# Split q and k parts copied straight from their tile to the stacks, in a ring of three tiles, with an opening in its own order

## The chip, the cores and the metric

The kernel runs on one core of a Trainium2 chip. Times are microseconds (us) of the device. The core has a matrix engine (TensorE, PE in the rows, with its weight loads as PEld), VectorE (DVE), ScalarE (ACT), GpSimd (POOL) and SyncE (SP), which computes nothing and issues transfers. Engines run their own instruction lists in order and wait for each other by semaphores. Transfers (DMA) from SP's queue and from ACT's queue are moved by 16 DMA engines.

## The reference, cut to what matters

Eight sequences of 512 tokens with 256 features. Causal attention with 16 heads of 16 dims, a layer norm, then a routed feed-forward layer (8 experts, each takes 129 tokens of each sequence) and a second layer norm. The change is in how q and k get ready for the scores.

```python
k = proj(W_key)
q = proj(W_query)          # (x @ W.T).reshape(b, t, h, hd).transpose(0, 2, 1, 3) * inv_sqrt_c
v = proj(W_value)
scores = jnp.einsum('bhqd,bhkd->bhqk', q, k) * hd ** (-0.5)
scores = jnp.where(causal, scores, -jnp.inf)
weight = jax.nn.softmax(scores, axis=-1)
out = jnp.einsum('bhqk,bhkd->bhqd', weight, v)
```

## The kernel before, in words

Two programs follow each other: `attention` (up to 491 us) and `experts`. Only `attention` is touched.

For each sequence b, q and k are made in four tiles of 128 rows (dims) by 512 tokens. Tile 4b+n: n % 2 is 0 for q and 1 for k, n // 2 is the half of the heads (8 heads). A `qk` stage is one tile: six passes of 512 columns on PE (L676) into a bank; ACT copies the bank twice, to the first bf16 part (L455) and to fp32, `qk_f` (L456); then POOL (L384 to L386; for sequence 0 DVE, L521 to L523) makes the second and third bf16 parts out of what is left. The three parts are in `parts`, a ring of two tiles that lies in the memory of an expert's second weight matrix (`w_raw` in the rows, as `xt` and `qk_f` do, which lie in that of the first). What is left over after the first part goes through a buffer of its own, `qk_r`.

A score needs for each head its 16 dims times six products of parts as 96 rows: the stacks `qst` and `kst` (`w_parts` in the rows). SP writes the three parts of each tile to DRAM, `part_d` (L316, 3 transfers of 128 KB), and a `stack` stage, which is a half of a sequence, reads them back into the stacks (L327, 12 transfers of 128 KB, each into 16 partitions, in rows of 1 KB). ACT may not write a part before the tile two before has landed in DRAM (`parts_out`, L454).

From the stacks come the `nat` units (L642: scores by query, whose maximum DVE takes in L510; 44 units a sequence, the first 22 need half 0) and the `st` units (L627: scores by key, exponentials by ACT in L430, masked by POOL). `nm` takes the maxima of a half of the heads to three rows of `qst`: DVE cuts them (L540 to L543), PE transposes (L704), ACT copies and issues a transfer of 24 KB from SBUF to SBUF (L470).

The order on all engines is that of `steps()`. An iteration i is 40 slots (g, k), g from 0 to 3, k from 0 to 9: slot (g, k) has an `st` unit of sequence i, one or two `nat` units three quarters of a sequence ahead, and what `STAGES` lists as (g, k, stage, how many sequences ahead, n). The tiles of sequence i+2 stand in slots (0,2), (1,0), (1,7) and (2,2), `stack` for its half 0 in (2,1), for half 1 in (0,1) of the next iteration, and `split`, which cuts the input `xt` of sequence i+3 on ACT (L437) and POOL (L389), in (3,5). SP loads the next `xt` right after `split` (L292). Before a `stack` SP waits until the `st` units of two sequences earlier, in the same half, are done (L323). What comes before iteration 0, the opening, is the same table run with i from -3, where `STARTED` leaves out what has been put in by hand.

PE has two banks each for `st` units and for stages, and three for `nat` units.

## Time and profile before

| | us |
|---|---|
| median of three runs | 966.62 |
| lowest and highest | 963.53, 967.97 |
| the profiled execution | 969.03 |
| its span, first to last instruction | 967.3 |

The span is the one that the rows below show; 1.7 us of the profiled execution lie outside it. In the rows, L12 is line 12 of the kernel before, "x6" a count of instructions, and "[2.58 <-DMA part_d<-w_raw]" says that the engine was idle for 2.58 us ahead of this instruction and what ended it. PEclk is the clock granted to TensorE, 1.00 being 2.4 GHz and 0.50 being 1.2 GHz.

### The profile page before, as it was taken

The page shows a single profiled execution, that of the slowest core. Times are in us where ns is not written, and L with a number is a line of the kernel's source. Part 1 is how long each engine was busy: PE and PEld are TensorE (multiplying, and loading weights), DVE is VectorE, ACT ScalarE, POOL GpSimd, SP SyncE. Part 2 cuts the span into 40 slices and gives each one's busy share as a digit, 9 for nine tenths or more (in the row PEclk, how much of TensorE's full clock was granted, in tenths as well). Part 3 has the DMA queues.
Part 4 walks back from the last instruction along what each step waited for, and adds up shares of the span by engine and source line. Part 5 has one row for each costly group of instructions (what it writes and reads, how often), then busy time and mean ns, then how long its engine had stood idle before and what let it go on. Part 6 is the DMA issues. An engine that isn't in the chain of part 4 may idle for free. (4 is left out here: it accounts for less than half of the span.)

```text
span 967.3 us, 17022 instructions
## 1 busy us (share of the span) xinstructions
PE 836.3 (86%) x5864; PEld 627.4 (65%) x5864; DVE 660.6 (68%) x2017; ACT 520.5 (54%) x1010; POOL 523.2 (54%) x622
## 2 busy tenths in 40 slices
PE   4769999999999999977666999998989899898990
PEld 3444454545455454433365989998989899898990
DVE  4467788787878788999759945555474735546464
ACT  2137666666675757544354445564545556454555
POOL 5347565656565653323655256757375645637344
PEclk9769999999999999988878899999999999998996
DMA  4996767687787778201052224325242332422248
GB/s 140 171 172 122 126 125 149 119 144 140 143 144 144 121 143 177 67 2 45 24 200 81 45 42 89 91 40 131 35 125 45 92 64 51 120 34 33 39 125 257
DMA packets 90102, 100.52 MB, mean 104 GB/s; under 512 B 8736, under 2 KB 83488, under 8 KB 89888
## 3 DMA queue, kind: packets, MB, share of 16 engines
q1 hardware_dynamic: 72560, 77.92, 37.6%
q0 software_dynamic: 12800, 16.92, 10.5%
q10 hardware_dynamic: 4656, 4.59, 1.5%
q8 instruction: 47, 0.77, 0.3%
q14 instruction: 39, 0.32, 0.1%
HBM read 65.38 MB, written 33.62 MB: 102 GB/s over the span
## 5 line engine op out<-in xcount | busy, mean ns | idle before, releaser
L510 DVE CUSTOM_DVE_ANT_0 n_ps<-n_ps,tri 128x512 f32<-128x512 f32 (+3 forms) x512 | 238.5, 517 | 75.3 <-PE n_ps L642 73.8
L1080 DVE TENSOR_TENSOR h_lo<-g,h_hi 128x384 fp32r<-128x384 f32 (+1 forms) x184 | 155.2, 851 | 126.3 <-ACT h_hi L1016 126.0
L430 ACT ACTIVATE pt<-st_ps 128x512 f32<-128x512 f32 x320 | 183.9, 601 | 76.0 <-PE st_ps L627 60.9
L1156 PE MATMUL y_ps<-w_parts,h_hi 128*128 128x256 f32 (+1 forms) x1152 | 213.3, 280 | 0.0
L1011 ACT ACTIVATE g<-h_ps,b 128x384 f32<-128x384 f32 (+1 forms) x192 | 104.2, 543 | 197.8 <-PE h_ps L1142 194.9
L1142 PE MATMUL h_ps<-tt_hi,w_parts 128*128 128x384 f32 (+1 forms) x768 | 179.1, 338 | 32.1 <-issue 21.5
L375 POOL TENSOR_SCALAR_AFFINE_SELECT pt<-pt 128x256 f32<-128x256 f32 (+1 forms) x320 | 111.6, 365 | 130.8 <-ACT pt L430 129.8
L1156 PEld LDWEIGHTS y_ps<-w_parts,h_hi 128*128 128x128 f32 (+1 forms) x1152 | 172.4, 178 | 3.3 <-ACT h_hi L1016 0.2
L983 POOL DMA_INDIRECT acc<-y,tok_no x64 | 102.3, 1599 | 120.6 <-DVE y L1094 112.4
L1156 PE MATMUL y_ps<-w_parts,h_lo 128*128 128x256 f32 (+1 forms) x576 | 161.0, 280 | 0.0
L1142 PEld LDWEIGHTS h_ps<-tt_hi,w_parts 128*128 128x128 f32 x768 | 133.6, 200 | 34.4 <-issue 33.2
L642 PE MATMUL n_ps<-w_parts 96*128 96x512 bf16 (+3 forms) x512 | 127.7, 314 | 15.1 <-DVE nmax L510 12.2
L627 PE MATMUL st_ps<-w_parts 99*128 99x512 bf16 (+3 forms) x512 | 127.0, 310 | 14.2 <-ACT pt L430 12.4
L1156 PEld LDWEIGHTS y_ps<-w_parts,h_lo 128*128 128x128 f32 (+1 forms) x576 | 102.4, 178 | 2.0
L659 PE MATMUL av_ps<-pt,vaug 128*32 128x512 f32 (+3 forms) x1024 | 97.6, 456 | 1.5 <-POOL pt L375 1.5
L1016 ACT ACTIVATE h_hi<-g 128x384 fp32r<-128x384 f32 (+1 forms) x192 | 94.4, 491 | 7.4
L627 PEld LDWEIGHTS st_ps<-w_parts 99*128 99x128 bf16 x512 | 42.6, 99 | 82.8 <-ACT pt L430 49.6
L1142 PE MATMUL h_ps<-tt_lo,w_parts 128*128 128x384 f32 (+1 forms) x384 | 96.1, 333 | 0.0
L642 PEld LDWEIGHTS n_ps<-w_parts 96*128 96x128 bf16 x512 | 44.7, 100 | 49.9 <-DVE nmax L510 34.8
L952 POOL DMA_INDIRECT tok<-x,tok_no x58 | 57.9, 999 | 32.9 <-DVE left_no L1071 16.4
L975 POOL TENSOR_TENSOR w_parts<-w_raw,w_parts 128x2048 fp32r<-128x2048 f32 x14 | 67.6, 4868 | 13.0 <-ACT w_parts L1024 13.0
L510 DVE DVE_READ_ACCUMULATOR2_ANT nmax<- 128x1 f32 x512 | 71.5, 140 | 0.0
(157 smaller groups left out, 1106.1 us busy)
## 6 DMA issues: line engine op xcount, KB each, us to landing
w_parts<-part_d SPq DMA_DIRECT2D x192, 128.0 KB, 6.1
w_raw<-in_w SPq DMA_DIRECT2D x16, 1024.0 KB, 5.6
part_d<-w_raw SPq DMA_DIRECT2D x96, 128.0 KB, 6.1
w_raw<-in_xt SPq DMA_DIRECT2D x8, 512.0 KB, 5.0
res<-in_x SPq DMA_DIRECT2D x8, 512.0 KB, 10.1
x<-res SPq DMA_DIRECT2D x8, 512.0 KB, 7.0
acc<-res SPq DMA_DIRECT2D x8, 512.0 KB, 8.2
fin<-acc SPq DMA_DIRECT2D x4, 512.0 KB, 3.9
```

The costliest lines, as they stand in the source:

```text
L375: nc.gpsimd.affine_select(out=x, in_=x, compare_op=ALU.is_ge, fill=0.0, base=0, pattern=[[0, len(tiles)], [1, P]], channel_multiplier=-1). ...
L430: nc.scalar.activation(pt[:, slot % PT_RING, n % UP, :], st_ps[at % ST_RING][:, :], ACT.Exp, scale=S_SCALE).then_inc(exp_done, 1)
L510: ins = nc.vector.tensor_tensor_reduce(out=src[:, h, :], in0=src[:, h, :], in1=mask, scale=-1.0, scalar=-BIG_NEG, op0=ALU.add, op1=ALU.min ...
L627: ins = nc.tensor.matmul(st_ps[at % ST_RING][:, c:c + T - kb * P], kst[0:KM, b % 2, h, kb * P:(kb + 1) * P], qst[0:KM, b % 2, h, kb * P:T] ...
L642: ins = nc.tensor.matmul(bank[:, j * w:(j + 1) * w], qst[0:KQ, b % 2, h, qb * P:(qb + 1) * P], kst[0:KQ, b % 2, h, 0:w], start=True, stop= ...
L659: ins = nc.tensor.matmul(av_ps[VW * j:VW * (j + 1), n * P:T], vaug[:, seq % 3, n, h, :], pt[:, (seq * PAIRS + h // 2) % PT_RING, u, c:c + ...
L983: nc.gpsimd.indirect_dma_start(acc_d[:, :], bass.IndirectOffsetOnAxis(ap=choice(e, j), axis=0), y[0:rows_of(j), j, :], None, compute_op=AL ...
L1011: nc.scalar.activation(g[:, at % G_RING, 0:cols], h_ps[at % H_RING][:, 0:cols], ACT.Gelu, bias=b1[:, e, n:n + 1]).then_inc(g_done, 1)
L1016: nc.scalar.activation(h_hi[:, q % 2, n, 0:cols], g[:, at % G_RING, 0:cols], ACT.Copy).then_inc(g_hi, 1)
L1080: nc.vector.tensor_tensor(h_lo[:, q % 2, n, 0:cols], g[:, at % G_RING, 0:cols], h_hi[:, q % 2, n, 0:cols].bitcast(F32), ALU.subtract).then ...
L1142: ins = nc.tensor.matmul(h_ps[at % H_RING][:, 0:cols], w[e % 2][:, k, units], x[:, q % TOK_RING, k, 0:cols], start=i == 0, stop=i == len(t ...
L1156: ins = nc.tensor.matmul(y_ps[at % Y_RING][0:rows, 0:C], x[:, q % 2, m, toks], w[e % 2][:, m, :], start=i == 0, stop=i == len(terms) - 1)
```

## The change

1. `part_d`, its 96 writes and the semaphores `parts_out` go. The host sorts the columns of the query and key weights by dim first, then head, inside each half. So the 128 rows of a tile are 16 groups of 8 heads, and a part can go from the tile to 16 partitions of a stack in one transfer. `stack` issues the same 12 transfers of 128 KB, with a tile in SBUF as their source: first the six of part 0 (as soon as ACT has made it), then the other six.
2. `parts` becomes a ring of three tiles (`part_of`; one part of nine has a buffer of its own, `last_part`). ACT may write into it when all 12 transfers of the stack that holds the tile three before have landed.
3. The rest is cut in place: subtract, copy to bf16, subtract (before: subtract, subtract, subtract).
4. In `STAGES` tile 1 moves from (1,0) to (1,2), and tile 3 from (2,2) to (3,1). The load of `xt` is a stage of its own, `xin`, in the place it had.
5. The opening is written out in `opening()` and `OPENING`.

```diff
-ST_RING, N_RING, PT_RING = 2, 3, 4
+ST_RING, N_RING, PT_RING, PART_RING = 2, 3, 4, 3
...
-    (1, 0, 'qk', 2, 1),
     (1, 0, 'onorm', -1, 3),
     (1, 1, 'nmcut', 0, 1),
+    (1, 2, 'qk', 2, 1),
...
-    (2, 2, 'qk', 2, 3),
...
+    (3, 1, 'qk', 2, 3),
...
     (3, 5, 'split', 3, 0),
+    (3, 5, 'xin', 4, 0),
...
+OPENING = {
+    5: (("qk", 1, 0),),
+    2 * N_QUARTER - 1: (("nmcut", 0, 0), ("nm", 0, 0), ("qk", 1, 1), ("stack", 1, 0), ("xin", 2, 0)),
+    2 * N_QUARTER + 3: (("qk", 1, 2),),
+    2 * N_QUARTER + 6: (("v", 1, 0), ("v", 1, 1), ("v", 1, 2), ("v", 1, 3)),
+    3 * N_QUARTER - 1: (("qk", 1, 3),),
+}
...
+    yield "split", 0, 0
+    yield "xin", 1, 0
+    for stage, n in (("qk", 0), ("qk", 1), ("stack", 0), ("centre", 0), ("qk", 2), ("v", 0), ("v", 1), ("v", 2), ("v", 3), ("qk", 3)):
+        yield stage, 0, n
+    yield "split", 1, 0
+    yield "stack", 0, 1
+    yield "fold", 0, 0
+    for n in range(NAT_LEAD * N_QUARTER):
+        yield "nat", 0, n
+        if n in OPENING:
+            yield from OPENING[n]
+    yield "split", 2, 0
+    yield "xin", 3, 0
...
+        j = 3 * (tile % PART_RING) + i
+        return most_parts[:, j, :] if j < 2 * KH * C // T else last_part[:, :]
...
+    def wait_stacked(engine, tile):
+
+        b, half_ = tile // 4, tile % 4 // 2
+        engine.wait_ge(stack_in[half_][b % 2], 16 * BLOCKS * (b // 2 + 1))
...
-                for which, stack, blocks in ((0, qst, Q_PARTS), (1, kst, K_PARTS)):
-                    for at, part in enumerate(blocks):
-                        src = part_d[which, b % 2, part, n, :, :].rearrange("(h d) n -> d h n", d=D)
-                        sp.dma_start(stack[at * D:(at + 1) * D, b % 2, HH * n:HH * (n + 1), :], src).then_inc(stack_in[n][b % 2], 16)
+                for first in (True, False):
+                    for which, stack, blocks in ((0, qst, Q_PARTS), (1, kst, K_PARTS)):
+                        tile = 4 * b + 2 * n + which
+                        if first:
+                            sp.wait_ge(qk_first, tile + 1)
+                        else:
+                            sp.wait_ge(qk_rest, tile + 1)
+                        for at, part in enumerate(blocks):
+                            if (part == 0) == first:
+                                sp.dma_start(stack[at * D:(at + 1) * D, b % 2, HH * n:HH * (n + 1), :],
+                                             part_of(tile, part)).then_inc(stack_in[n][b % 2], 16)
...
-                link(nc.gpsimd.tensor_tensor(qk_r[:, :], qk_f[:, tile % 2, :], parts[:, tile % 2, 0, :], ALU.subtract))
-                link(nc.gpsimd.tensor_tensor(parts[:, tile % 2, 1, :], qk_f[:, tile % 2, :], parts[:, tile % 2, 0, :], ALU.subtract))
-                nc.gpsimd.tensor_tensor(parts[:, tile % 2, 2, :], qk_r[:, :], parts[:, tile % 2, 1, :], ALU.subtract).then_inc(qk_rest, 1)
+                left, mine = qk_f[:, tile % 2, :], [part_of(tile, i) for i in range(3)]
+                link(nc.gpsimd.tensor_tensor(left, left, mine[0], ALU.subtract))
+                link(nc.gpsimd.tensor_copy(mine[1], left))
+                nc.gpsimd.tensor_tensor(mine[2], left, mine[1], ALU.subtract).then_inc(qk_rest, 1)
...
-                    act.wait_ge(parts_out[tile % 2], 48 * (tile // 2))
-                nc.scalar.activation(parts[:, tile % 2, 0, :], ps[:, :], ACT.Copy).then_inc(qk_first, 1)
+                if tile >= PART_RING:
+                    wait_stacked(act, tile - PART_RING)
+                nc.scalar.activation(part_of(tile, 0), ps[:, :], ACT.Copy).then_inc(qk_first, 1)
```

What this does to the order, at the two places that matter. First SP at the start of the opening, tiles 0 to 3 of sequence 0, with the semaphores that each transfer waits for. Before:

```order
7 L316 DMA part_d<-w_raw 128x512 [waits qk_rest,qk_first]
8 L316 DMA part_d<-w_raw 128x512 x2
9 L316 DMA part_d<-w_raw 128x512 [waits qk_rest,qk_first]
10 L316 DMA part_d<-w_raw 128x512 x2
11 L327 DMA w_parts<-part_d 16x8x512 [waits parts_out1,parts_out0]
12 L327 DMA w_parts<-part_d 16x8x512 x11
```

After:

```order
7 L347 DMA w_parts<-w_raw 16x8x512 [waits qk_first]
8 L347 DMA w_parts<-w_raw 16x8x512 x2
9 L347 DMA w_parts<-w_raw 16x8x512 [waits qk_first]
10 L347 DMA w_parts<-w_raw 16x8x512 x2
11 L347 DMA w_parts<-w_raw 16x8x512 [waits qk_rest]
12 L347 DMA w_parts<-w_raw 16x8x512 x2
13 L347 DMA w_parts<-w_raw 16x8x512 [waits qk_rest]
14 L347 DMA w_parts<-w_raw 16x8x512 x2
```

The writes to DRAM and the wait for both tiles are gone; the first three copies wait for ACT's first copy alone.

Second ACT in iteration 1, from slot (1,4) on (`nmt` is the copy of `nm`, `o_t` that of `ot`, `vaug` with `scores` that of a `v`, `pt` an exponential; L455 and L479 are the first copy of a tile). Before:

```order
92 L455 ACTIVATE w_raw<-stage_ps 128x512
93 L456 ACTIVATE w_raw<-stage_ps 128x512
94 L430 ACTIVATE pt<-st_ps 128x512 x5
95 L455 ACTIVATE w_raw<-stage_ps 128x512
96 L456 ACTIVATE w_raw<-stage_ps 128x512
97 L430 ACTIVATE pt<-st_ps 128x512 x3
98 L463 ACTIVATE vaug<-stage_ps 128x16x16
```

After:

```order
92 L479 ACTIVATE w_raw<-stage_ps 128x512
93 L480 ACTIVATE w_raw<-stage_ps 128x512
94 L453 ACTIVATE pt<-st_ps 128x512 x8
95 L487 ACTIVATE vaug<-stage_ps 128x16x16
...
108 L503 ACTIVATE lge<-lg 128x32
109 L453 ACTIVATE pt<-st_ps 128x512 x2
110 L479 ACTIVATE w_raw<-stage_ps 128x512
```

The last tile of a sequence is copied behind the four `v` instead of ahead of them, and the exponentials of the slots after (3,1) stand behind that copy.

## Rows read from the trace of the kernel before

**Rows 1.** The page: the span.

```profile
span 967.3 us, 17022 instructions
```

**Rows 2.** Stages: length, busy us (instructions) of each engine, PEclk, DMA share, GB/s.

```profile
24.00:48.00 24.00, 17.05 (x68) 11.66 (x67) 10.61 (x41) 4.47 (x11) 9.27 (x7) 0.73 1.11 172
48.00:72.00 24.00, 16.52 (x69) 9.59 (x68) 15.74 (x69) 7.42 (x17) 10.01 (x10) 0.63 0.96 171
...
165.30:215.60 50.30, 48.12 (x352) 25.52 (x352) 41.43 (x174) 32.96 (x67) 30.77 (x55) 1.00 0.75 138
...
491.40:967.30 475.90, 419.67 (x3030) 407.57 (x3030) 279.66 (x544) 248.97 (x479) 261.52 (x179) 0.93 0.37 86
```

**Rows 3.** Timeline of the opening: start, us, engine, line, what it writes and reads.

```profile
13.55 0.60 ACT L455 ACTIVATE w_raw<-st_ps 128x512 bf16<-128x512 f32 x1 [5.60 <-PE st_ps L676]
...
20.61 0.17 DVE L529 TENSOR_TENSOR w_lo<-rw,w_hi 128x16 fp32r<-128x16 f32 x1
...
22.23 5.53 SPq L327 DMA_DIRECT2D w_parts<-part_d  x12
...
32.43 1.05 PE L676 MATMUL stage_ps<-xt_lo,w_hi 128*128 128x512 f32 x2
33.28 1.05 PE L676 MATMUL stage_ps<-xt_hi,w_lo 128*128 128x512 f32 x2
...
35.89 0.59 PE L642 MATMUL n_ps<-w_parts 96*128 96x512 bf16 x1 [1.55 <-DMA w_parts<-part_d]
...
36.52 0.70 DVE L510 CUSTOM_DVE_ANT_0 n_ps<-n_ps,tri 128x512 f32<-128x512 f32 x1 [10.93 <-PE n_ps L642]
36.62 0.60 ACT L455 ACTIVATE w_raw<-stage_ps 128x512 bf16<-128x512 f32 x1 [7.81 <-DMA part_d<-w_raw]
...
51.52 0.60 ACT L455 ACTIVATE w_raw<-stage_ps 128x512 bf16<-128x512 f32 x1 [11.36 <-DMA part_d<-w_raw]
...
52.66 0.81 PE L684 MATMUL stage_ps<-w_hi,xt_hi 128*128 128x264 f32 x2 [3.79 <-ACT w_raw L456]
...
70.10 0.14 DVE L510 DVE_READ_ACCUMULATOR2_ANT nmax<- 128x1 f32 x1
...
71.14 1.41 PE L676 MATMUL stage_ps<-xt_hi,w_hi 128*128 128x512 f32 x2
```

**Rows 4.** DMA in five short stretches; columns as in rows 2.

```profile
28.00:34.00 6.00, 2.56 (x6) 1.82 (x6) 0.00 (x0) 0.81 (x1) 2.34 (x1) 0.68 1.15 133
318.00:329.00 11.00, 11.00 (x84) 6.10 (x84) 8.83 (x37) 7.36 (x14) 6.98 (x15) 1.00 1.16 127
169.20:171.80 2.60, 2.60 (x22) 0.54 (x20) 1.98 (x8) 2.11 (x5) 1.86 (x2) 1.00 1.17 152
130.20:131.00 0.80, 0.46 (x6) 0.11 (x3) 0.77 (x3) 0.00 (x0) 0.72 (x2) 1.00 1.09 370
111.90:112.40 0.50, 0.50 (x10) 0.21 (x3) 0.44 (x2) 0.50 (x2) 0.29 (x1) 1.00 0.17 49
```

**Rows 5.** Timeline of iteration 2: SP, PE and ACT around the moved tiles.

```profile
165.69 0.37 SPq L292 DMA_DIRECT2D w_raw<-in_xt  x1
...
166.18 5.61 SPq L327 DMA_DIRECT2D w_parts<-part_d  x12
...
178.01 0.38 PE L642 MATMUL n_ps<-w_parts 96*128 96x512 bf16 x1
...
193.84 5.79 SPq L327 DMA_DIRECT2D w_parts<-part_d  x12
...
205.94 0.34 PE L642 MATMUL n_ps<-w_parts 96*128 96x384 bf16 x1
...
206.93 0.39 PE L642 MATMUL n_ps<-w_parts 96*128 96x512 bf16 x1 [0.39 <-DVE nmax L510]
```

**Rows 6.** Groups, the page's and then 97 to 366 us alone: busy us, mean ns, idle before.

```profile
L510 DVE CUSTOM_DVE_ANT_0 n_ps<-n_ps,tri 128x512 f32<-128x512 f32 (+3 forms) x512 | 238.5, 517 | 75.3 <-PE n_ps L642 73.8
...
L384 POOL TENSOR_TENSOR w_raw<-w_raw 128x512 f32<-128x512 f32 x21 | 24.3, 1158 | 38.9 <-ACT w_raw L456 29.4 <-ACT w_raw L455 9.6
```

More of the change, by code:

```diff
@@ L93 @@
 ROUND_AT += [(B, place) for place in (1, 5, 12, 16)]
-STARTED = [(-2, stage, n) for stage in ("qk", "v", "stack") for n in range(4)]
-STARTED += [(-1, "stack", 0), (-1, "nmcut", 0), (-1, "nm", 0)]
 AV_PLACES = (4, 5, 6, 7)
@@ L99, with opening @@
 BY_DVE = ("onorm", "proj", "pick", "picked")
+OPENING = {
[5 more added lines that the diff above has]
+}
+def opening():
+    yield "split", 0, 0
[11 more added lines that the diff above has]
+    yield "xin", 3, 0
 def steps():
-    for i in range(-3, B + 1):
+    yield from opening()
+    for i in range(B + 1):
         for g in range(4):
@@ L118, in steps @@
                     yield "av", group, AV_PLACES.index(k)
-                if (i, g, k) == (-2, 0, 0):
-                    for stage, n in (("qk", 0), ("qk", 1), ("stack", 0), ("centre", 0), ("qk", 2), ("qk", 3), ("v", 0), ("v", 1), ("v", 2), ("v", 3)):
-                        yield stage, 0, n
-                if (i, g, k) == (-1, 2, 0):
-                    yield "fold", 0, 0
                 for gg, kk, stage, ahead, n in STAGES:
-                    if (gg, kk) == (g, k) and 0 <= i + ahead < B and (i, stage, n) not in STARTED:
+                    if (gg, kk) == (g, k) and 0 <= i + ahead < B:
                         yield stage, i + ahead, n
-                        if (i, stage, n) == (-1, "qk", 1):
-                            yield "stack", 1, 0
                 place = 10 * g + k
@@ L269, in attention @@
     bases = sem("bases")
-    part_d = nc.dram_tensor("part_d", [2, 2, 3, 2, P, T], BF16).ap()
     act_no, dve_no = numbers(BY_ACT), numbers(BY_DVE)
@@ L298, in _ @@
         for stage, b, n in steps():
-            if stage == "split" and b + 1 < B:
-                sp.wait_ge(x_split, b + 1)
-                load_xt(b + 1)
-                if b == 0:
+            if stage == "xin":
+                sp.wait_ge(x_split, b)
+                load_xt(b)
+                if b == 1:
                     sp.dma_start(wpn[:, :, :], wpn_d.rearrange("(k p) n -> p k n", p=P)).then_inc(wpn_in, 16)
@@ L331, in _ @@
                     sp.wait_ge(qk_rest, 4 * B)
+                    for half_ in range(2):
+                        wait_stacked(sp, 4 * (B - 1) + 2 * half_)
                     sp.dma_start(ahead["w1_raw"][:, :, :], w1_d[0].rearrange("(k p) n -> p k n", p=P)).then_inc(ahead["w1_in"], 16)
@@ L518, in _ @@
                     dve.wait_ge(qk_rest, n)
[L519 to L523 removed]
+                left, mine = qk_f[:, n % 2, :], [part_of(n, i) for i in range(3)]
+                link(nc.vector.tensor_tensor(left, left, mine[0], ALU.subtract))
+                link(nc.vector.tensor_copy(mine[1], left))
+                nc.vector.tensor_tensor(mine[2], left, mine[1], ALU.subtract).then_inc(qk_rest, 1)
             elif stage == "centre":
```

29 lines of the change are left out of this document (6 added, 23 removed).

## The prediction

> **What bounds the kernel now.** First the page's head and a table of stages [rows 1, 2]: of a span of 967.3 us, the experts take 475.9 from 491.4 on, and nothing in them is touched. In an iteration in the middle of the attention (165.3 to 215.6 us) PE is busy for 48.1 of 50.3 us at full clock: PE is the bound, with about 2 us of idle time an iteration. DVE has 41.4, ACT 33.0, POOL 30.8. The 16 DMA engines are used at 0.75, and no engine waits for a transfer there. In the opening it is otherwise: from 24 to 72 us PE is busy for 33.6 of 48 us, at a clock of 0.73 and 0.63, and the DMA share is 1.11 and 0.96.
>
> Then the timeline of the opening [rows 3]. The reader is to see three waits. The first stack is read from 22.23 us on, and PE's first `nat` unit gets it at 35.89, so DVE makes its first maximum only at 36.52. ACT waits 7.81 and 11.36 us for parts to land in DRAM, behind stack transfers in the same queue. While it does, PE waits 3.79 us for a stage bank. DVE ends the 33 units of the opening at 70.24, and PE begins the first tile of sequence 2, the first work that needs the next input, at 71.14.
>
> Last the transfers [rows 4, 5]: they decide what the new wait of ACT costs.
>
> **The change, part by part.**
>
> *Less traffic.* 96 writes of 128 KB go, 12.6 MB. In the middle nobody waits for them, so they are worth nothing there beyond what they take from the queue ahead of stacks. In the opening they are the waits of 7.81 and 11.36 us.
>
> *The stack transfers themselves.* Twelve are left, with another source. In stretches in which the queue holds stack reads, the engines move 133, 127 and 152 GB/s with all 16 busy; rows of the same 1 KB size for `res`, which go to 128 partitions, run at 370 GB/s [rows 4]. So it is neither the size of the rows nor DRAM as a source that makes them slow, and what is left that sets them apart is that 16 partitions take them. That speaks for the same rate when the source is SBUF. At 128 KB each: 0.86 us at 152 GB/s, 0.99 at 133, 1.03 at 127. The one copy from SBUF to SBUF, that of `nm`, speaks for more: 24 KB on 3 of 16 engines (share 0.17) at 49 GB/s [rows 4], which is 16 GB/s an engine where a stack read gives 8 to 9.5. It is short, though, and may end before whatever slows the others fills up. From first issue to release the first stack took 35.89 - 22.23 = 13.7 us, of which 12 x 0.99 = 11.9 are transfers and 1.8 start and completion [rows 3, 4]. I take release = first issue + 1.8 + 12 d, with d = 0.86 us: with the part writes gone the queue holds less beside the stacks, as in the stretch with 152 GB/s. The ends of d are SP's issue at 5.6 / 12 = 0.47 [rows 5] and 1.03.
>
> The Trainium skill bears on this twice. "SBUF — State Buffer", section "Door 1: The DMA port swizzle", says that a transfer's bandwidth goes by how many of 16 ports its partitions reach; 16 partitions in a row reach four of them, a quarter of 436 GB/s, an estimate of 109 GB/s and 1.2 us for each transfer. By that rule every wait below would be 2 to 4 us longer. "DMA: Bandwidth & Descriptors", section "Where 436 GB/s comes from", says that copies inside SBUF are held by the fabric at 435 GB/s and not by memory; by that the transfers would keep up with SP. The rows at 127 to 152 GB/s stand near the first, the `nm` copy nearer to the second.
>
> *The new wait of ACT, tile 1 in slot (1,2).* It needs the stack of half 1 of the sequence before. Iteration 2 [rows 5]: SP issues `xt` at 165.69, the stack from 166.18. `xt` goes first in the queue, 512 KB at 370 GB/s, 1.4 us, of which 0.5 is SP's own distance: 0.9. Release: 166.18 + 0.9 + 1.8 + 12 x 0.86 = 179.2. ACT wants the tile when PE has done it: the unit of slot (1,2) ends at 178.2, 1.6 us of that was the tile which now stands behind it, so PE again ends at 178.2, and ACT comes at 178.3. Wait 0.9 us. Behind it on ACT are the exponentials of slot (1,3) and on; PE has two banks and some 0.4 us of other work ahead. Cost 0.5 us. At d = 0.99 it is 2.0, at 1.03 2.5, under 0.78 nothing. It comes in iterations 1 to 4; in iteration 5 no `xt` goes ahead and there is hardly a wait. In iteration 0 the stack is issued only after `split` of sequence 2, later against the slots: 2 us (0 to 4).
>
> *Tile 3 in slot (3,1)* needs half 0 of its own sequence, issued at 193.84: release 193.84 + 1.8 + 10.3 = 205.9. PE ends the unit of (3,1) at 206.1, ACT comes at 206.2: no wait. At d = 0.99 it is 1.3 us, at 1.03 1.8, in each of 6 iterations. Tiles 0 and 2 need stacks that have landed by then (tile 2: five slots behind tile 1).
>
> Sum of the waits at 0.86: 4 x 0.5 + 2 = 4 us.
>
> *The moved tiles.* PE's work is the same. At (3,1) PE now waits for DVE twice, 0.39 us (at 206.93) and about as much two units later; a tile of 1.4 us there fills these, and POOL, without a tile at (2,2), gives DVE its `rstd` sooner. Against that DVE, busy for 41 of 50 us, has less time at (2,2). Where ACT's wait stops PE, DVE catches up too. I take -0.5 us for each of 6 iterations, -3 (0 to -6).
>
> *Cutting in place.* One POOL subtraction of 1.16 us [rows 6] becomes a cast. Bound: 0 to -1.1 us for each tile on POOL, which is not the bound. It is counted only in the opening's DVE chain, at nothing.
>
> *The opening.* The first stack copies go out when ACT has made tile 0's first part, at 13.55 + 0.60 = 14.15 instead of 22.23; the last three need DVE's cut of tile 1, which stands ahead of L529 (20.61) in DVE's order, so all twelve are out by about 21 [rows 3]. From 15 on (the first input and weight loads are ahead of them; I take 1 us for that) the stack needs 10.3 us and 1.1 to complete: 26.5, or 28 at d = 0.99. That isn't what comes last now. The four `v` stand ahead of tile 3 and wait for L529, which ends at 20.78. A pair of passes of 512 columns at half clock starts 0.85 us after the one before (32.43, 33.28), so a tile is 2.9 us with its end, a `v` with 264 columns 1.3; at full clock half of that, 1.45 and 0.7. PE is through tile 3 at 25.5 to 29. ACT's three copies, 2.2 us, and POOL's part of `split`, 2.35 as for twice the columns of [rows 6], line two, give the next input at 30 to 33.6; before, PE had it at 31.4: no gain. DVE cuts tile 3 and begins its maxima at about 31.5, 5 us sooner than at 36.52. The 33 units are 12 heads; 128 heads took 238.5 us [rows 6], 1.86 each, 22.3. DVE is stopped three times by PE's new order: by tile 0 of sequence 1, by the transpose of the maxima with tile 1 in a row, and by four `v` in a row: at full clock some 1.6 + 2.6 + 1.8 us, at half clock 1.6 + 4.1 + 4.1, with 1.2 for cutting the maxima. It ends at 31.5 + 22.3 + 1.2 + 6.0 = 61.0, or 64.8, against 70.24. But the last tile now stands at the very end: PE 1.4, ACT 1.1, POOL three steps of 1.16, less for the cast, 3.1, then POOL's 2.35. So the first tile of sequence 2 can start at 61.0 + 8.0 = 69.0, against 71.14. Gain 2 us; at half clock it is a loss of 2, and with fewer stops a gain of 5. What is late next is POOL with tile 3 and `split`.
>
> **Sum.** -2 (opening) - 3 (moved tiles) + 4 (ACT's waits) = -1: 969.03 - 1 = 968.0 in an execution like the profiled one, whose span and 1.7 us around it move together. That execution is 2.4 us above the median; in terms of the median 965.6, and I say 965.5. Its own range is 960 to 971.
>
> **The rivals.**
>
> *A, the copies inside SBUF keep up with SP.* d is under 0.75, ACT never waits for a stack. For it: the `nm` copy at twice the rate an engine, and `res` at 370 GB/s. Against it: 16 receiving partitions as before. The opening is then worth 3 and the moved tiles 3.5. Time: -6.5, so 962.5 and 960.1 by the median; range 956 to 963.
>
> *B, slower: ACT's wait for the stack becomes the bound.* d is 0.99 to 1.03, as most of the stack reads show. The wait at (1,2) costs 2.0 to 2.5 in four iterations and 3.5 in iteration 0, 12.5 in all; that at (3,1) 1.3 to 1.8 in six, 9; sum 21.5. Less 5 for idle time of PE and DVE that these stops swallow and 2 for the opening: +14.5, so 983.5 and 981 by the median; range 971 to 990. It decides from about d = 0.88 us, where the waits are worth more than the gains. For it: [rows 4], lines one and two. Against it: the line with 152 GB/s.
>
> *C, the opening gains nothing.* PE's gaps keep the clock at 0.5 as in [rows 2], and POOL's chain at the end eats the rest: 3 to 4 us more than forecast, 969 by the median; range 965 to 973.
>
> **How the numbers follow.** Chances: forecast 0.36, A 0.27, B 0.28, C 0.09. A measurement of this kernel can tell about 0.5% from no change, 4.8 us: faster is below 961.8, slower above 971.5. Faster: A 0.24, forecast 0.09: 0.33. Slower: B 0.28, C 0.02, forecast 0.03: 0.33. The same: 0.34. The likeliest is the forecast's 965.5. Range 956 to 984: it holds all but the far end of B and some of A.
>
> **What would show it.** In the trace of the changed kernel: DVE's first maximum at 31 to 32 us; no wait of ACT for a stack in the opening beyond 1 us; the first tile of sequence 2 on PE at 69. In iterations 1 to 4 ACT's first copy of tile 1 "<-DMA w_parts" with about 1 us, tile 3 with none; 2.4 and 1.3 us or more mean B, none at all means A. An iteration, 50.3 us before [rows 2], should be 50.3 again, 50 for A and 53 for B. The GB/s while stack copies alone are in the queue give d directly. The experts should take 475.9 us again; if they don't, the forecast is wrong in a place that it doesn't look at.

## The result, and the profile after

| | us |
|---|---|
| changed kernel, median of four runs | 996.79 (995.29 to 1003.04) |
| kernel before, beside it | 966.19 |
| ratio | 1.0331, 95% interval 1.0281 to 1.0381 |
| span of the profiled execution, before and after | 967.3, 995.0 |

The change makes the kernel slower by 3.3%, and the time is outside the range of 956 to 984. The page of the changed kernel, its span and two of the groups of [rows 6]:

```profile
span 995.0 us, 16861 instructions
...
L534 DVE CUSTOM_DVE_ANT_0 n_ps<-n_ps,tri 128x512 f32<-128x512 f32 (+3 forms) x512 | 239.0, 519 | 102.9 <-PE n_ps L665 100.8
...
L407 POOL TENSOR_TENSOR w_raw<-w_raw 128x512 f32<-128x512 f32 x28 | 32.4, 1157 | 98.5 <-ACT w_raw L479 72.6
```

The work costs what it did (maxima 519 ns for 517, the subtraction 1157 ns for 1158), but DVE now waits 100.8 us for PE's `nat` units, where it waited 73.8. The stages, to be held against [rows 2] (length, busy us and count of PE, PEld, DVE, ACT, POOL, then PEclk, DMA share, GB/s); the third is an iteration, 50.30 us long before, and the last ends the experts:

```profile
24.00:48.00 24.00, 17.11 (x69) 10.51 (x69) 16.36 (x53) 4.92 (x13) 5.26 (x4) 0.71 0.95 107
48.00:72.00 24.00, 16.12 (x77) 10.04 (x78) 13.47 (x60) 7.38 (x18) 7.54 (x8) 0.78 0.51 72
...
179.36:235.78 56.42, 50.50 (x356) 26.57 (x352) 40.32 (x172) 32.83 (x67) 28.63 (x54) 0.94 0.63 95
...
520.00:995.00 475.00, 418.89 (x3030) 406.83 (x3030) 277.81 (x544) 249.43 (x479) 262.54 (x179) 0.93 0.36 86
```

Two marks in both traces place the loss: ACT's first copy of the first tile of sequence 2, and its `nmt` copy in slot (3,4) of iteration 5, called the mark from here on (the expectations below speak of the last maxima). Behind the mark lie what is left of the attention and the experts.

| | before | after | difference |
|---|---|---|---|
| start to first tile of sequence 2 | 74.30 | 78.71 | +4.4 |
| from there to the mark | 287.30 | 311.33 | +24.0 |
| from the mark to the end | 605.70 | 604.96 | -0.7 |

The iterations lose most. ACT's waits between 72 and 395 us (engine, line, waited for: us, times, longest):

```profile
ACT w_raw L479 <- DMA w_parts<-w_raw: 21.1, 4, 7.9
...
ACT w_raw L479 <- DMA w_parts<-last_part: 10.2, 2, 6.2
```

These are the six first copies of tile 1 in slot (1,2), 31.4 us together, one in each of the iterations 0 to 5. One of them, with SP, ACT and PE in order of time (against [rows 5]), and then the stretches around it:

```profile
182.86 0.37 SPq L316 DMA_DIRECT2D w_raw<-in_xt  x1
183.34 5.10 SPq L347 DMA_DIRECT2D w_parts<-w_raw  x8
...
191.76 0.60 SPq L332 DMA_DIRECT2D res<-in_x  x1
...
200.83 0.60 ACT L479 ACTIVATE w_raw<-stage_ps 128x512 bf16<-128x512 f32 x1 [6.12 <-DMA w_parts<-w_raw]
...
202.46 0.61 PE L650 MATMUL st_ps<-w_parts 99*128 99x512 bf16 x1 [4.19 <-ACT pt L453]
```

```profile
195.00:200.00 5.00, 3.27 (x24) 1.58 (x22) 3.66 (x17) 0.00 (x0) 0.19 (x1) 1.00 1.14 132
200.00:203.00 3.00, 0.54 (x2) 0.13 (x2) 0.00 (x0) 2.17 (x5) 0.95 (x1) 0.82 0.30 82
203.00:206.00 3.00, 3.00 (x15) 1.21 (x14) 0.76 (x2) 0.93 (x2) 2.83 (x6) 0.50 0.03 8
206.00:209.00 3.00, 3.00 (x18) 1.46 (x16) 0.62 (x2) 1.26 (x3) 0.41 (x1) 0.55 0.00 0
```

The reader is to see a chain of four. The stack lands 17.5 us after its first issue; ACT, which came at 194.7, does nothing until then; PE stands still for 4.19 us behind ACT's exponentials; and when it starts again, the granted clock is at 0.50, 1.2 GHz, for some 6 us. So the stop is paid for again: PE is busy for 50.50 us in this iteration, where the same work takes 47.60 in the run with a ring of four below. Not all of ACT's 6.12 us is the stack's. PE finishes the tile only at 196.2, and in the ring of four ACT waits at the same copy, for PE alone:

```profile
181.74 0.60 ACT L481 ACTIVATE w_raw<-stage_ps 128x512 bf16<-128x512 f32 x1 [1.56 <-PE stage_ps L701]
```

The opening, against [rows 3]:

```profile
13.73 6.92 POOL L420 MEMSET w_parts<- 3x8192 f32 x1
...
14.29 20.12 SPq L347 DMA_DIRECT2D w_parts<-w_raw  x20
...
15.59 5.35 DVE L545 CAST w_raw<-w_raw 128x512 bf16<-128x512 f32 x1
...
21.76 0.60 ACT L479 ACTIVATE w_raw<-st_ps 128x512 bf16<-128x512 f32 x1 [5.33 <-DVE w_raw L546]
...
30.64 0.60 ACT L479 ACTIVATE w_raw<-st_ps 128x512 bf16<-128x512 f32 x1 [1.10 <-DMA w_parts<-w_raw]
...
32.81 2.34 POOL L412 TENSOR_TENSOR xt_lo<-w_raw,xt_hi 128x1024 fp32r<-128x1024 f32 x1 [12.16 <-ACT xt_hi L460]
32.99 2.71 DVE L546 TENSOR_TENSOR w_raw<-w_raw 128x512 bf16<-128x512 f32 x1
...
35.71 0.68 DVE L534 CUSTOM_DVE_ANT_0 n_ps<-n_ps,tri 128x512 f32<-128x512 f32 x1
...
69.06 0.60 ACT L479 ACTIVATE w_raw<-stage_ps 128x512 bf16<-128x512 f32 x1 [5.03 <-DMA w_parts<-last_part]
...
75.78 1.19 PE L699 MATMUL stage_ps<-xt_hi,w_hi 128*128 128x512 f32 x2 [3.14 <-POOL xt_lo L412]
```

The first copies do go out at 14.29, as predicted. But DVE's cast of 512 columns takes 5.35 us (0.43 us for the next one), so tile 2 is copied at 21.76 (at 17.57 in the run without casts below); a subtraction takes 2.71 instead of 0.69; and at the end ACT waits 5.03 us for stack (1,0) before it may write the last tile. The first maximum is at 35.71, not 31.5, and the first tile of sequence 2 on PE at 75.78, not 69. That GpSimd's memset holds a cast on DVE could have been read from the kernel before. There the cast of 128x16 ended at 20.57 and the memset at 20.54; in the changed kernel the same cast, behind the memset, takes 0.17 us.

```profile
13.61 6.93 POOL L397 MEMSET w_parts<- 3x8192 f32 x1
...
19.54 1.03 DVE L528 CAST w_hi<-rw 128x16 fp32r<-128x16 f32 x1
```

### The profile page after: what moved, and what is told of

Same layout as the page of the kernel before. It is cut to its first block and busy times, and to the rows that moved or that the text cites. A ratio compares the mean times of both kernels' runs of the same rounds, so it can differ in the third digit from the quotient of the medians.

```text
span 995.0 us, 16861 instructions
## 1 busy us (share of the span) xinstructions
PE 839.2 (84%) x5864; PEld 626.2 (63%) x5864; DVE 657.0 (66%) x2017; ACT 519.9 (52%) x1010; POOL 508.5 (51%) x622
## 3 DMA queue, kind: packets, MB, share of 16 engines
q10 hardware_dynamic: 4656, 4.59, 1.4%
## 5 line engine op out<-in xcount | busy, mean ns | idle before, releaser
L534 DVE CUSTOM_DVE_ANT_0 n_ps<-n_ps,tri 128x512 f32<-128x512 f32 (+3 forms) x512 | 239.0, 519 | 102.9 <-PE n_ps L665 100.8
L1103 DVE TENSOR_TENSOR h_lo<-g,h_hi 128x384 fp32r<-128x384 f32 (+1 forms) x184 | 132.4, 728 | 126.8 <-ACT h_hi L1039 126.6
L665 PE MATMUL n_ps<-w_parts 96*128 96x512 bf16 (+3 forms) x512 | 128.6, 316 | 17.5 <-DVE nmax L534 15.6
L682 PE MATMUL av_ps<-pt,vaug 128*32 128x512 f32 (+3 forms) x1024 | 101.5, 472 | 2.0 <-POOL pt L398 2.0
L407 POOL TENSOR_TENSOR w_raw<-w_raw 128x512 f32<-128x512 f32 x28 | 32.4, 1157 | 98.5 <-ACT w_raw L479 72.6
L665 PEld LDWEIGHTS n_ps<-w_parts 96*128 96x128 bf16 x512 | 44.7, 100 | 52.2 <-DVE nmax L534 37.9
```

Of the source, the lines that this page charges most:

```text
L534: ins = nc.vector.tensor_tensor_reduce(out=src[:, h, :], in0=src[:, h, :], in1=mask, scale=-1.0, scalar=-BIG_NEG, op0=ALU.add, op1=ALU.min ...
L665: ins = nc.tensor.matmul(bank[:, j * w:(j + 1) * w], qst[0:KQ, b % 2, h, qb * P:(qb + 1) * P], kst[0:KQ, b % 2, h, 0:w], start=True, stop= ...
L682: ins = nc.tensor.matmul(av_ps[VW * j:VW * (j + 1), n * P:T], vaug[:, seq % 3, n, h, :], pt[:, (seq * PAIRS + h // 2) % PT_RING, u, c:c + ...
L1103: nc.vector.tensor_tensor(h_lo[:, q % 2, n, 0:cols], g[:, at % G_RING, 0:cols], h_hi[:, q % 2, n, 0:cols].bitcast(F32), ALU.subtract).then ...
```

## The experiments

The theory after the traces, **W**: the loss is ACT's wait for a stack, in slot (1,2) above all. Rivals: **T**, the copies inside SBUF slow the engines or each other; **M** or its opposite, that the moved tiles cost or bring something; and for the size of the wait, whether source, order, receiving partitions or rows set the rate of a copy.

**A ring of four tiles.** The fourth lies in a buffer that `attention` doesn't use until its end.

```diff
-ST_RING, N_RING, PT_RING, PART_RING = 2, 3, 4, 3
+ST_RING, N_RING, PT_RING, PART_RING = 2, 3, 4, 4
...
+        if j >= 9:
+            return ahead["tok0"][:, :, :].rearrange("p a c -> p (a c)").bitcast(BF16).rearrange("p (j n) -> p j n", n=T)[:, j - 9, :]
```

> The changed kernel with a ring of four tiles of parts instead of three, so that a tile waits for the stack that holds the same tile of the sequence before, which has landed long ago. Theory W (the loss is ACT's wait for a stack): in the changed kernel these waits are 7.93, 6.23, 6.12, 4.59, 4.01 and 2.48 us at tile 1 and 5.03 us at the last tile of the opening, and 23.8 us were lost between the start of iteration 0 and the last maxima. Without the waits an iteration is back at 50 to 50.5 us (53.8, 55.3, 56.4, 54.7 with them) and the time is about 970, or 967 if the opening gets back its 4 to 5 us too. Rival T (the traffic itself: copies inside SBUF slow PE, DVE or ACT): the waits go but an iteration stays at 53 or more, time 985 to 995. The rate of the copies should not change under either.

Measured: 965.89, ratio 0.9993 (0.9978 to 1.0008). No wait of ACT for a stack is left, and an iteration (columns as above) is

```profile
214.16:263.46 49.30, 47.60 (x356) 25.58 (x352) 40.32 (x172) 32.85 (x68) 28.64 (x54) 1.00 0.73 109
```

W holds, T falls. Since both kernels begin the iterations at the same time (`split` of sequence 2 at 70.28), the price of each wait can be read by itself. The length goes from one `split` to the next, the last one to the mark:

| iteration | 0 | 1 | 2 | 3 | 4 | 5 |
|---|---|---|---|---|---|---|
| ACT's wait in the changed kernel | 7.93 | 6.23 | 6.12 | 4.59 | 4.01 | 2.48 |
| at the same copy in the ring of four, for PE's tile | 1.34 | 1.55 | 1.56 | 1.55 | 1.55 | 1.55 |
| length, changed kernel | 53.79 | 55.29 | 56.42 | 54.73 | 51.50 | 48.03 |
| length, ring of four | 45.22 | 49.33 | 49.33 | 49.30 | 49.32 | 47.40 |
| price of the wait | 8.6 | 6.0 | 7.1 | 5.4 | 2.2 | 0.6 |
| of which PE is busy for longer | -0.4 | 1.6 | 2.9 | 2.8 | 0.1 | 0.1 |
| PEclk, changed kernel | 0.87 | 0.97 | 0.94 | 0.94 | 1.00 | 1.00 |
| PEclk, ring of four | 0.86 | 1.00 | 1.00 | 1.00 | 1.00 | 1.00 |

31.4 us of waits cost 29.9, of which 1.9 in iteration 0 come before its wait (the first tile of sequence 2 is at 78.71 instead of 76.84, late from the opening). The stack's own share of a wait is row one less row two. In iterations 1 to 5 the price is that share, less 0.37 us that PE has in hand, plus what PE's work takes longer at the lower clock. So a share of 2.46 us costs 2.2 in iteration 4, at full clock, and one of 3.04 costs 5.4 in iteration 3, of which 2.8 is clock.

**Another order of the copies.** From sequence 1 on, neighbours go to different blocks of 16 partitions.

```diff
+                if b:
+                    sp.wait_ge(qk_rest, 4 * b + 2 * n + 2)
+                    for which, at in ((0, 0), (0, 1), (0, 4), (0, 5), (1, 0), (1, 1), (1, 4), (1, 5), (0, 2), (0, 3), (1, 2), (1, 3)):
...
```

 Theory O (each copy is held by the ports of its 16 partitions, and neighbours overlap only where these differ): the first issue of a stack to ACT's release falls from 15.3 to 17.6 us to 12 or less, the waits at tile 1 from 4 to 8 us to 0 to 3, and the time from 996.8 to 972 to 985. Rival F (a copy is slow by itself, by the source or by the size of its rows, and they go one after another): 15 to 17.6 us again and a time within 3 us of 996.8.

Measured: 996.92, 1.0320 (1.0297 to 1.0344). The time is rival F's, and a miss for theory O; but two things hide in it. In the opening stack (1,0) now waited for the cut of both its tiles, and ACT for it 11.53 us instead of 5.03. Behind that the iterations were 5.5 us shorter. The run was repeated without that part, the spread order only from stack (1,1) on:

> The changed kernel with the copies of a stack in the spread order, for stack (1,1) and all later ones; the first three stacks as in the changed kernel. In the first run of that order the opening lost 7 us, because stack (1,0) then waited for the cut of tile 1, and the iterations gained 5.5 (319.8 to 314.2 us from the last `split` of the opening to the last maxima). Theory: the gain alone, 5 to 6 us, time 990 to 993. Rival: no gain, 996 to 998.

Measured: 989.99, 1.0223 (1.0163 to 1.0283), at the edge of the theory's 990 to 993. The waits at (1,2) sum to 28.8 instead of 31.4. One iteration, with a wait of 4.79 us, keeps its clock:

```profile
176.92:229.16 52.24, 47.65 (x356) 25.60 (x352) 40.31 (x172) 32.70 (x67) 28.58 (x54) 1.00 0.65 103
```

The next, with 5.86 us, takes 54.81 at 0.97. From the last `split` of the opening to the mark this kernel is 5.6 us shorter than the changed one; 2.6 of it is waiting, and in iterations 1 to 4 PE is busy for 2.6 us less, which is clock. The order itself is worth about half a microsecond a stack.

**The copies by themselves.** Twelve copies of 128 KB behind the kernel's last instruction, one series after the other:

> The kernel before, and behind its last instruction eight series of twelve transfers of 128 KB with nothing else running, each series waited for before the next: from SBUF in the changed kernel's order of blocks; from SBUF in the order of the kernel before (0, 16, 32, 48, 64, 80, twice); from DRAM in that order; from DRAM in the changed kernel's order; from SBUF in the order 0, 16, 64, 80, 0, 16, 64, 80, 32, 48, 32, 48; from SBUF with all twelve into the same 16 partitions; from DRAM likewise; from SBUF into 128 partitions. Theory O (ports of the receiving partitions, overlap only between neighbours that differ): about 14 to 15 us for all twelve into the same partitions whatever the source, 10 to 12 in the order of the kernel before, less in the spread order, 13 to 15 in the changed kernel's order, 4 to 8 into 128 partitions. Theory S (the source makes the difference): 14 to 15 for every series from SBUF and 10 to 11 for every one from DRAM. Rival R (a rate of 0.86 us a copy as I predicted, slower in the changed kernel only because other traffic shares the queue): 10 to 11 us for all the series into 16 partitions.

The time from the first issue of a series to that of the next, which waits for all twelve, and the rate in its middle:

| into | from | order of blocks | us | GB/s |
|---|---|---|---|---|
| 16 partitions | SBUF | changed kernel's | 15.3 | 118 |
| 16 | SBUF | kernel before's | 14.8 | 121 |
| 16 | DRAM | kernel before's | 13.8 | 130 |
| 16 | DRAM | changed kernel's | 13.7 | 133 |
| 16 | SBUF | spread | 14.9 | 123 |
| 16 | SBUF | all the same | 16.7 | 105 |
| 16 | DRAM | all the same | 16.5 | 105 |

Two of these series in the trace (columns as in [rows 4]), in turn and all into the same 16 partitions:

```profile
976.00:982.00 6.00, 0.00 (x0) 0.00 (x0) 0.00 (x0) 0.00 (x0) 0.00 (x0) 0.50 1.16 118
...
1045.00:1055.00 10.00, 0.00 (x0) 0.00 (x0) 0.00 (x0) 0.00 (x0) 0.00 (x0) 0.50 1.17 105
```

No theory is right as a whole. The source makes 1.0 or 1.6 us of 15 and, where all copies go to the same partitions, 0.2; the order makes half a microsecond, and the same partitions every time make 2. In the first 1.5 us in which a series moves data, stretches of half a microsecond reach 190 to 242 GB/s, and the rest runs at 105 to 133, so a rate from the first microseconds of a stack is too high. Two queues at once:

> The kernel before, and behind its last instruction six series of twelve copies of 128 KB from SBUF into 16 partitions, issued half by SyncE's queue and half by ACT's: one block of partitions each (0 and 16; then 0 and 80; then 0 and 0), the six blocks in turn on both, and blocks 0, 64, 32 against 16, 80, 48; at the end all twelve on SyncE's queue, in turn. On one queue twelve copies took 14.8 us in turn and 16.7 into the same partitions. Theory K (the receiving ports bound it): two blocks of different ports at once take 8 to 10 us, the same block twice 16 to 17. Rival J (the 16 DMA engines bound it, each row costs its time whatever its partition): 14 to 17 us for all.

```profile
970.00:980.00 10.00, 0.00 (x0) 0.00 (x0) 0.00 (x0) 0.00 (x0) 0.00 (x0) 0.50 1.15 121
...
999.00:1011.00 12.00, 0.00 (x0) 0.00 (x0) 0.00 (x0) 0.00 (x0) 0.00 (x0) 0.50 1.16 105
```

The first row is partitions 0 to 15 from one queue and 16 to 31 from the other, 15.0 us; the second is 0 to 15 from both, 16.7 us. With the six blocks in turn on both queues it was 115 GB/s. K's 8 to 10 us didn't come. The number of receiving partitions and the length of the rows:

> The kernel before, and behind its last instruction five series of twelve copies of 128 KB from SBUF on SyncE's queue: into 16 partitions (128 rows of 1 KB, six blocks in turn, as before: 14.8 us); into 32 partitions, then 64, then 128, the same rows of 1 KB; last into 16 partitions again in rows of 4 KB, read from 32 partitions. Theory K (ports of the receiving partitions): 32 partitions take 8 to 9 us, 64 no less, 128 9 as measured (there SyncE issues no faster), rows of 4 KB 14 to 16. Rival R (each row of 1 KB costs an engine its time): 32 and 64 partitions 14 us as well, rows of 4 KB 8 to 10.

```profile
972.00:981.00 9.00, 0.00 (x0) 0.00 (x0) 0.00 (x0) 0.00 (x0) 0.00 (x0) 0.50 1.15 121
986.00:994.00 8.00, 0.00 (x0) 0.00 (x0) 0.00 (x0) 0.00 (x0) 0.00 (x0) 0.50 1.14 143
999.00:1006.00 7.00, 0.00 (x0) 0.00 (x0) 0.00 (x0) 0.00 (x0) 0.00 (x0) 0.50 1.16 154
1010.00:1016.00 6.00, 0.00 (x0) 0.00 (x0) 0.00 (x0) 0.00 (x0) 0.00 (x0) 0.50 0.59 198
1021.00:1029.00 8.00, 0.00 (x0) 0.00 (x0) 0.00 (x0) 0.00 (x0) 0.00 (x0) 0.50 1.05 130
```

16, 32, 64 and 128 partitions in rows of 1 KB, then 16 in rows of 4 KB: 14.9, 12.9, 12.2 and 9.3 us for the first four. Up to 64 partitions all engines are busy; at 128 they are busy for 0.59 only, and SP, at 0.64 us a copy, is the bound. Long rows bring little. So what holds a copy goes with how many partitions receive it, but not in proportion, and what it is stays open.

**Cutting without a cast**, on DVE (shown) and likewise on GpSimd:

```diff
-                link(nc.vector.tensor_tensor(left, left, mine[0], ALU.subtract))
-                link(nc.vector.tensor_copy(mine[1], left))
+                link(nc.vector.tensor_tensor(mine[1], left, mine[0], ALU.subtract))
+                link(nc.vector.tensor_tensor(left, left, mine[0], ALU.subtract))
```

> The changed kernel with the rest cut by three subtractions again, in place (second part = left - first, then left = left - first, then the third), so that no engine casts. Theory L (DVE's cast of 5.35 us at 15.59 in the changed kernel waits for GpSimd's memset, which ends at 20.65; a subtraction there took 0.69 us in the kernel before): the cast's place takes 0.7 us, the first copy of tile 2 on ACT comes at 17 to 18 instead of 21.76, the first maximum at 31 to 32 instead of 35.71. The time falls by 0 to 4 us, less if the opening is then held by ACT's wait for stack (1,0). Rival (the cast waits for something else, a semaphore or a late input): the same 5 us stand at the first subtraction.

Measured: 1000.62, 1.0366 (1.0337 to 1.0395).

```profile
15.72 0.69 DVE L545 TENSOR_TENSOR w_raw<-w_raw 128x512 f32<-128x512 f32 x1
...
17.57 0.60 ACT L479 ACTIVATE w_raw<-st_ps 128x512 bf16<-128x512 f32 x1 [0.76 <-PE st_ps L699]
...
30.14 0.60 ACT L479 ACTIVATE w_raw<-st_ps 128x512 bf16<-128x512 f32 x1 [3.79 <-DMA w_parts<-w_raw]
...
32.76 2.71 DVE L546 TENSOR_TENSOR w_raw<-w_raw 128x512 bf16<-128x512 f32 x1
...
35.48 0.68 DVE L534 CUSTOM_DVE_ANT_0 n_ps<-n_ps,tri 128x512 f32<-128x512 f32 x1
```

Theory L is right on the cast: in its place stands 0.69 us, and tile 2 comes at 17.57. It is wrong on the maximum, 35.48. The 4 us are waited away at tile 3, which needs the first stack, landed 15.7 us after its first issue. The time, forecast to fall by up to 4 us, didn't: the median is 3.8 us above the changed kernel's, and the two intervals overlap. The waits at (1,2) were 33.4 us instead of 31.4; why they are longer is open.

**Tile 1 later, in the ring of three.**

```diff
-    (1, 2, 'qk', 2, 1),
...
-    (1, 7, 'qk', 2, 2),
+    (1, 6, 'qk', 2, 1),
...
+    (2, 2, 'qk', 2, 2),
```

> The changed kernel, its ring of three and its opening, with tile 1 in slot (1,6) instead of (1,2) and tile 2 in (2,2) instead of (1,7). A stack is landed some 15.5 to 18 us after its `xt` is issued, ACT comes to slot (1,2) at 11.9 us, and a slot is 1.23 us. Theory W (only the wait in the wrong place costs): at (1,6) the wait is 0 to 1.5 us, an iteration 49.3 to 50.5, time 966 to 972, with the opening's loss still in it. Rival (what stands behind the tiles is then late: the third stage bank's turn, `stack` in (2,1), GpSimd): an iteration is 51 or more, time 976 or more.

Measured: 971.20, 1.0023 (0.9999 to 1.0047). A wait of 3.14 us is left in iteration 0 and none later, and an iteration takes 49.80 us. From the last `split` of the opening to the mark it is 295.5 us, against 319.8 in the changed kernel and 289.9 with the ring of four: four slots give back 24 of the 30 us, without any memory. With the opening's two small mends beside it:

> As the last, with DVE's three subtractions and with the input of sequence 2 loaded behind stack (0,1). Both mend something in the opening that ACT's waits for stacks cover in a ring of three (3.79 us at tile 3 of sequence 0 and 5.55 at the last tile, in the run without casts). Theory C (covered): within 2 us of the run before it. Rival: the opening gains 3 to 6 us as with the ring of four.

Measured: 969.21, 1.0020 (0.9996 to 1.0043): covered, as expected. The first tile of sequence 2 is copied at 78.09 instead of 78.56.

**One part alone on the kernel before.** The moved tiles:

```diff
+        table = STAGES if i < 0 else MOVED
```

> The kernel before, parts through DRAM, with tile 1 in slot (1,2) and tile 3 in slot (3,1) from iteration 0 on, nothing else. With the ring of four an iteration takes 49.33 us against 50.35 in the kernel before. Theory M (the moved tiles are the cause): 49.3 to 49.5 here too, time 960 to 963. Rival N (it is the cast on GpSimd, 0.61 for 1.16 us, or the 96 writes that are gone): 50.3 us, time 965 to 968.

Measured: 963.37, 0.9944 (0.9918 to 0.9970).

```profile
211.84:261.17 49.33, 47.63 (x356) 25.59 (x352) 40.36 (x172) 32.84 (x67) 30.67 (x55) 1.00 0.76 141
```

The moved tiles alone take 1.0 us off an iteration, with all the traffic through DRAM still there (141 GB/s against 109 above). Theory M; the 12.6 MB and the cast are worth nothing there. What the moved tiles give can be read from DVE, which is busy for 40.36 us instead of 41.46. Before, GpSimd cut tile 1 (from 178.39 to 182.11 in iteration 2) while DVE cut the maxima for `nm`, and two small casts waited; with tile 1 in (1,2) GpSimd comes to it later. Before, then here:

```profile
178.81 0.77 DVE L540 CAST nm<-nmax 128x32 bf16<-128x32 f32 x1
...
179.84 1.02 DVE L542 CAST nm<-nmax_r 128x32 bf16<-128x32 f32 x1
```

```profile
228.49 0.18 DVE L575 CAST nm<-nmax 128x32 bf16<-128x32 f32 x1
...
228.93 0.18 DVE L577 CAST nm<-nmax_r 128x32 bf16<-128x32 f32 x1
```

PE's waits for maxima, the gain that the prediction named, fall from 0.8 to 0.4 us an iteration. How much of the 1.0 us is one and how much the other no run tells, since both tiles were moved together. Then the order of the opening:

> The kernel before, parts through DRAM and a ring of two, with the changed kernel's order of the opening, nothing else. Theory G (the order itself holds the opening: one tile at the very end and the input of sequence 2 loaded behind stack (1,0)): the first tile of sequence 2 is copied 2 to 5 us later than in the kernel before (74.30), time 968 to 972. Rival H (the order is sound, and what the changed kernel lost there is its cast and its ring of three): 74 or earlier, time 961 to 967.

Measured: 981.46, 1.0116 (1.0069 to 1.0164), worse than expected.

```profile
70.24 0.43 SPq L308 DMA_DIRECT2D w_raw<-in_xt  x1
...
79.66 1.06 ACT L453 ACTIVATE xt_hi<-w_raw 128x1024 fp32r<-128x1024 f32 x1 [11.86 <-DMA w_raw<-in_xt]
```

The new order puts the load of sequence 2's input behind stack (1,0) in SP's list, and SP waits there for that stack's tiles. In the changed kernel ACT's wait for the stack covers it; with the ring of four it shows as 2.36 us.

**A mended opening, with the ring of four.** DVE cuts without the cast, tile 3 stands ahead of the four `v`, and the load of the input behind stack (0,1).

```diff
-    for stage, n in (("qk", 0), ("qk", 1), ("stack", 0), ("centre", 0), ("qk", 2), ("v", 0), ("v", 1), ("v", 2), ("v", 3), ("qk", 3)):
+    for stage, n in (("qk", 0), ("qk", 1), ("stack", 0), ("centre", 0), ("qk", 2), ("qk", 3), ("v", 0), ("v", 1), ("v", 2), ("v", 3)):
...
     yield "stack", 0, 1
+    yield "xin", 2, 0
```

> The ring of four tiles, and the opening mended where its traces show waits: DVE cuts by three subtractions (no cast behind the memset), tile 3 of sequence 0 is made ahead of the four v (in the ring of four it needs no stack), and the input of sequence 2 is loaded behind stack (0,1) instead of behind stack (1,0). With the ring of four alone DVE's first maximum was at 35.75 us and ACT's copy of the first tile of sequence 2 at 76.84, against 36.52 and 74.30 in the kernel before. Theory P (the opening is a chain through DVE, begun by the first stack, which lands at about 30): first maximum at 30 to 31.5, the first tile of sequence 2 at 70 to 72, time 959 to 962. Rival Q (the end of the opening is set by the last tile and `split` and not by DVE's start): first maximum earlier but the first tile of sequence 2 at 75 or later, time 964 to 966.

Measured: 958.77, 0.9887 (0.9842 to 0.9931), first maximum at 30.53. Then also the tiles of sequence 1 spread over the opening:

```diff
...
+    3: (("qk", 1, 0),),
+    8: (("qk", 1, 1), ("stack", 1, 0)),
+    14: (("qk", 1, 2),),
+    18: (("qk", 1, 3),),
+    21: (("nmcut", 0, 0), ("nm", 0, 0)),
+    24: (("v", 1, 0), ("v", 1, 1)),
+    27: (("v", 1, 2), ("v", 1, 3), ("split", 2, 0), ("xin", 3, 0)),
```

> As the last, and the tiles of sequence 1 spread over the first 19 of the 33 units of the opening, the v and `split` of sequence 2 behind units 24 and 27, so that nothing but maxima stands at its end. Theory P: the opening ends with DVE's maxima, 22.3 us of units after a first maximum at 30 to 31 and 4 to 7 us of stops: 57 to 61; the first tile of sequence 2 is copied at 60 to 66 instead of 76.84, time 950 to 958. Rival Q2 (each tile stops DVE wherever it stands, since PE has three banks of maxima only): the stops are 10 us or more, the first tile at 68 or later, time 958 to 962.

Measured: 954.26, 0.9838 (0.9790 to 0.9886), theory P's time: 1.6% below the kernel before.

```profile
30.53 0.70 DVE L537 CUSTOM_DVE_ANT_0 n_ps<-n_ps,tri 128x512 f32<-128x512 f32 x1 [5.31 <-PE n_ps L668]
...
64.99 0.60 ACT L482 ACTIVATE w_raw<-stage_ps 128x512 bf16<-128x512 f32 x1 [1.66 <-PE stage_ps L702]
```

Last, the same slots and the same opening with the parts through DRAM:

> The kernel before with its parts through DRAM and its ring of two, with the moved tiles and with the opening that took 954.3 us with direct copies and a ring of four. It tells what the direct copies are worth once the rest is the same. Theory D (they save the way through DRAM ahead of the first stack, 36.5 against 30.5 us for the first maximum, and waits of 8 and 11 us of ACT for parts to land, which stand in the opening alone): the first tile of sequence 2 at 70 to 76 us instead of 64.99, time 958 to 966. Rival E (the opening's order alone was the gain): 953 to 957.

Measured: 962.49, 0.9944 (0.9924 to 0.9965).

```profile
56.67 0.60 ACT L472 ACTIVATE w_raw<-stage_ps 128x512 bf16<-128x512 f32 x1 [10.84 <-DMA part_d<-w_raw]
```

Through DRAM the better order of the opening brings nothing beyond the moved tiles (962.49 here, 963.37 for these alone), since ACT still waits 10.84 and 4.70 us for parts to land; the first tile of sequence 2 is copied at 72.61. The direct copies with their ring of four are worth 8.6 us of span (961.4 against 952.8) over the way through DRAM with its ring of two, 7.6 of it before the first tile of sequence 2. How much of that is the longer ring isn't shown: a longer ring with the parts through DRAM was not run, and ACT's 10.84 and 4.70 us are waits of a ring of two.

## Why the prediction was wrong, point by point

*What bounds the kernel, and the traffic:* right. PE is the bound in the middle, the experts take 475.00 us instead of 475.90, and 12.6 MB less are worth nothing in an iteration.

*The stack transfers:* the term that failed. d was taken as 0.86 us, with 1.03 as the upper end. With the 1.8 us of the formula, 15.3 us for twelve alone is 1.12 each, above that end. In the kernel ACT was released 17.6, 17.5, 16.0 and 15.4 us after the stack's first issue in iterations 1 to 4; less 0.9 and 1.8 that is a d of 1.24, 1.23, 1.11 and 1.06. Why the four differ by 2 us is open: `xt` ahead of the stack and `res` behind it stand in all of them. The row that I went by, 152 GB/s in [rows 4], is 2.6 us long and lies close behind the first issue; at about the same place (186 to 190 us) the changed kernel ran at 141. The other two rows, 127 and 133, were close to the steady rate from DRAM, and SBUF as a source is 1.0 to 1.6 us a stack slower, not equal.

Beside it stood a rule that I named and gave no chance. "SBUF — State Buffer", section "Door 1: The DMA port swizzle", of the Trainium skill gave an estimate of 1.2 us a copy. In the formula that is 17.1 us from the first issue of the stack, near the 17.5 of iterations 1 and 2 and above the 15.4 of iteration 4. Where all copies go to the same 16 partitions, the runs agree with its 109 GB/s (105). Over several blocks of partitions, on one queue or two, 115 to 123 were measured from SBUF and 130 to 133 from DRAM. It should have been a rival with a chance.

*The wait at (1,2):* the place and the mechanism were right, and it is rival B's, with 0.28. Counted from PE's tile, as in the forecast, the stack's share of the wait was 4.7, 4.6, 3.0 and 2.5 us in iterations 1 to 4, where 0.9 was forecast and B's d gives 2.5 to 2.9. In iteration 0 it was 6.6 instead of 2 (0 to 4). The price of a wait at full clock was right: the share less 0.4 was forecast, less 0.37 was measured. What I hadn't in the sum at all is the clock: behind the stop of 4.19 us it was at 1.2 GHz for 6 us, and in iterations 1 to 3 PE was busy for 1.6, 2.9 and 2.8 us longer. In place of +4 stand 29.9 us, of which 1.9 come from the opening.

*Tile 3 in slot (3,1):* no wait in any iteration, as forecast, but not for the reason given, and so by luck. The forecast had ACT come 12.4 us after the first issue. With the measured d its formula gives a release 14.5 to 16.7 us after it, and waits of 2 to 4 us. ACT came 17.6 us after it in iteration 2 (first issue 212.75, copy 230.36). The working had that distance 5 us too short.

*The moved tiles:* right in sign and range. -3 was forecast, 0 to -6; alone they gave -5.4 (-7.9 to -2.9). That DVE's casts no longer meet GpSimd's cut of tile 1 (1.4 us of DVE an iteration) wasn't in the working.

*Cutting in place, at nothing:* wrong in the opening. I named no cover for it and didn't look at what GpSimd does there. Its memset of 6.93 us stood in the trace of before, beside subtractions of 0.69 us, which it doesn't hold, and beside the small cast of 1.03 us, which it does.

*The opening:* -2 forecast (-5 to +2), +4.4 measured to the first tile of sequence 2. The first maximum was 4 us late because of the cast and, had that not been, because of the first stack (d again). Two waits of the new order were missing from the working: the last tile on ACT for stack (1,0), 5.03 us, and the input of sequence 2 behind that stack on SP. I had priced where an instruction stands for PE, ACT and DVE, and not for SP.

The sum, on the span: the ring of four, which has all of the change but these waits, stands at -3.6 (+2.5 to the first tile of sequence 2, -4.0 from there to the mark, -2.2 behind, rounded). The waits in the iterations add 29.9, and the part behind them differs by 1.4: 27.7, which is 995.0 less 967.3. Without the waits my sum of -5 (-2, -3) was near that -3.6, but partly by luck: the opening was 4.5 us worse than forecast, and 2.2 of the gain lie behind the mark, for which nothing was forecast.
